# Moving the next tile's input transposes into the attention block, and a bf16 cast from VectorE to ScalarE, in a post-norm transformer layer on 8 cores

## The reference

```python
qkv = x @ W_qkv.T + b_qkv
q, k, v = jnp.split(qkv, 3, axis=-1)
q = q * HD ** (-0.5)
# q, k, v in blocks of 64 tokens, per head
attn = softmax(einsum('bhnld,bhnmd->bhnlm', qb, kb))
out = einsum('bhnlm,bhnmd->bhnld', attn, vb) @ W_out.T + b_out
x = layernorm(x + out)
h = silu(x @ wg.T) * (x @ wu.T)        # wg, wu = int32 / 127, hidden 3072
x = layernorm(x + h @ wd.T)
```

## Time and profile before

| | us |
|---|---|
| profiled execution | 2746.69 |
| its span, slowest core (core 0) | 2745.1 |
| median of the two timed runs | 2869.86 |
| the two timed runs | 2765.27 and 2974.46 |
| PE busy | 2001.0 (73% of the span) |
| DVE busy | 817.2 (30%) |
| ACT busy | 436.5 (16%) |

### The profile page before, as it was taken

How to read it: one execution, slowest core, us unless ns; L and a number is a source line. 1 busy time by engine, 2 the same in 40 slices (tenths; PEclk the granted TensorE clock), 3 DMA queues, 4 the chain that set the end, 5 groups by cost and what they waited for, 6 DMA issues and landing times.

```text
span 2745.1 us, 27109 instructions; the slowest of 8 cores (2723.5 to 2745.1 us)
## 1 busy us (share of the span) xinstructions
PE 2001.0 (73%) x10416; PEld 1001.5 (36%) x10560; DVE 817.2 (30%) x1314; ACT 436.5 (16%) x835; POOL 66.7 (2%) x111
## 2 busy tenths in 40 slices
PE   1666239657897669867797669876698678976795
PEld 1433114224443334324443335334443244433342
DVE  2444001153213341053312441143311532133411
ACT  0111101012211112021211112011211122111110
POOL 2000000100000000000000000000000000000000
PEclk9967569867898769966899679977799678987798
DMA  9999993810252004400153003410043102420033
GB/s 187 161 113 119 243 239 113 191 46 16 74 156 77 31 16 116 146 37 25 39 162 107 16 31 92 146 54 31 16 149 113 46 17 80 152 75 16 24 115 107
DMA packets 258829, 253.54 MB, mean 92 GB/s; under 512 B 88608, under 2 KB 221744, under 8 KB 258128
## 3 DMA queue, kind: packets, MB, share of 16 engines
q1 hardware_dynamic: 216576, 121.65, 17.1%
q0 software_dynamic: 19280, 86.11, 14.2%
q10 hardware_dynamic: 22848, 44.05, 4.8%
HBM read 216.13 MB, written 56.62 MB: 99 GB/s over the span
## 4 chain that ended last, share of the span: by engine, by line
PE 57%; DVE 13%; DMA 10%; SPq 9%; issue 5%; another core or an unknown queue 3%; ACT 2%; DVEq 0%; POOL 0%; ACTq 0%; POOLq 0%
PE ps L783 23%; PE ps L389 8%; SPq L289 7%; PE ps L838 7%; DMA wdb<-wdT_s 5%; PE ps L579 5%; PE ps L423 3%; PE ps L472 3%; PE ps L466 3%; DMA wdb<-wd_nat 2%; DVE x L861 1%; DVE stats L880 1%; SPq L263 1%; DVE stats L640 1%
## 5 line engine op out<-in xcount | busy, mean ns | idle before, releaser
L783 PE MATMUL ps<-x1T,wgu 128*128 128x512 bf16 x3008 | 664.4, 381 | 98.3 <-DMA wgu<-wuT_s 93.5
L783 PEld LDWEIGHTS ps<-x1T,wgu 128*128 128x128 bf16 x3072 | 301.4, 98 | 459.6 <-issue 102.1
L838 PE MATMUL ps<-wdb,hT 128*128 128x512 bf16 x1504 | 348.1, 385 | 62.3 <-DMA wdb<-wdT_s 34.0
L801 DVE TENSOR_TENSOR hT<-silu,ps 128x512 bf16<-128x512 bf16 x192 | 132.0, 687 | 753.7 <-PE ps L783 629.4
L389 PE MATMUL ps<-xT,RWqkv 128*128 128x256 bf16 x2048 | 266.0, 298 | 23.9 <-DVE xT L371 23.6
L838 PEld LDWEIGHTS ps<-wdb,hT 128*128 128x128 bf16 x1536 | 147.1, 99 | 263.2 <-issue 103.6
L389 PEld LDWEIGHTS ps<-xT,RWqkv 128*128 128x128 bf16 x2048 | 204.5, 106 | 85.1 <-issue 28.2
L423 PE MATMUL ps<-RWqkv,xT 128*128 128x512 bf16 x496 | 142.7, 435 | 87.6 <-DVE vtok L435 58.6
L579 PE MATMUL ps<-RWout,aoT 128*128 128x512 bf16 x480 | 166.0, 505 | 47.8 <-DVE aoT L567 25.0
L795 ACT ACTIVATE silu<-ps 128x512 bf16<-128x512 f32 x192 | 114.6, 597 | 520.1 <-PE ps L783 520.0
L397 ACT ACTIVATE qkT<-ps,bqkvT_s 128x256 bf16<-128x256 f32 x256 | 121.4, 474 | 454.7 <-PE ps L389 454.5
(11 more groups left out here) (71 smaller groups left out, 1067.8 us busy)
## 6 DMA issues: line engine op xcount, KB each, us to landing
wgu<-wgT_s SPq DMA_DIRECT2D x64, 768.0 KB, 4.9
wgu<-wuT_s SPq DMA_DIRECT2D x64, 768.0 KB, 7.0
wdb<-wdT_s ACTq DMA_DIRECT2D x84, 512.0 KB, 3.7
xf<-x POOLq DMA_DIRECT2D x16, 1024.0 KB, 5.2
y<-x POOLq DMA_DIRECT2D x16, 1024.0 KB, 5.8
x<-wqkv POOLq DMA_DIRECT2D x24, 512.0 KB, 9.1
wg_nat<-wg POOLq DMA_DIRECT2D x1, 6144.0 KB, 64.1
wu_nat<-wu POOLq DMA_DIRECT2D x1, 6144.0 KB, 120.9
```

Of the source, the lines that this page charges most:

```text
L783: P.do("tensor", lambda tn, wi=wi, k=k, mi_=mi_, boff=boff, pair=pair: tn.matmul(pair[:, wi * 512:(wi + 1) * 512], wgu[:, boff + wi * (KCH ...
L801: P.do("vector", lambda v, m=m, pair=pair: v.tensor_tensor(hT[:, m * 512:(m + 1) * 512], silu2[:, (m % 2) * 512:(m % 2 + 1) * 512], pair[: ...
L838: P.do("tensor", lambda tn, m=m, l=l, half=half, wslot=wslot, coff=coff: tn.matmul(psl[l][:, half * 512:(half + 1) * 512], hT[:, m * 512 + ...
```

## The change

`front_a` is cut in two. Its first part, now `front_x` (the cast of x, the transposes, the evacuations to `xT`), is emitted for tile t+1 inside `tile_front(t)`, between `attn_A(0, 1)` and `attn_T(0, 0)`. Its second part, `front_q` (q and k), stays where `front_a` was. For tile 0 both run ahead of the loop. The added argument `wait_scores` is a wait of TensorE on its own count, and by the rule above it emits nothing. The second edit moves the cast of the normalised x (L698 before) from VectorE to ScalarE, as an ACTIVATE with Copy, and the waits that go with it.

```diff
-            def front_a(t):
+            def front_x(t, wait_scores=0):
...
+                    if st == 0 and wait_scores:
+                        w.append(("pe", wait_scores))
...
+            def front_q(t):
                 for c in range(16):
...
                 attn_A(0, 0)
                 attn_A(0, 1)
+                if t + 1 < n_tiles:
+                    front_x(t + 1, wait_scores=mil["scores", t, 0, 1])
                 attn_T(0, 0)
...
-                    P.do("vector", lambda v, xsl=xsl, st=st: v.tensor_copy(
-                        out=aoT[:, st * 1024:(st + 1) * 1024], in_=xsl),
-                        inc="ve",
-                        waits=[("ve!", mil["norm1", t, st]), ("pe", mil["wout", t, 1]),
+                    P.do("scalar", lambda sC, xsl=xsl, st=st: sC.activation(
+                        out=aoT[:, st * 1024:(st + 1) * 1024], in_=xsl, func=AF.Copy),
+                        inc="sc",
+                        waits=[("ve", mil["norm1", t, st]), ("pe", mil["wout", t, 1]),
                                ("sb5", mil.get("dump_aoT", 0))])
-                    mil["x1b", t, st] = P.c["ve"]
+                    mil["x1b", t, st] = P.c["sc"]
...
-            front_a(0)
+            front_x(0)
+            front_q(0)
...
-                    front_a(2 * s + 1)
+                    front_q(2 * s + 1)
...
-                    front_a(2 * s + 2)
+                    front_q(2 * s + 2)
```

More of the change, by code:

```diff
@@ L624, in tile_front @@
                 if EARLY_A and t + 1 < n_tiles:
-                    front_a(t + 1)
+                    front_x(t + 1)
+                    front_q(t + 1)
                 if STAGE <= 7:
@@ L710, in tile_front @@
                             inc="pe" if c == KCH - 1 else None,
-                            waits=(w + [("ve", mil["x1b", t, st])]) if c == 0 else ())
+                            waits=(w + [("sc", mil["x1b", t, st])]) if c == 0 else ())
                     mil["x1t_mm", t, st] = P.c["pe"]
```

## The result

| | kernel before | changed kernel |
|---|---|---|
| profiled execution, us | 2746.69 | 2708.24 |
| its span, slowest core | 2745.1 (core 0) | 2706.7 (core 2) |
| median of all runs | 2758.82 (10 runs) | 2708.8 (11 runs) |
| ratio, with its 95% interval | 1 | 0.9843 (0.9822 to 0.9864) |
| DVE busy | 817.2 | 796.2 |

The change saves 1.6%, clear of the measurement's scatter and less than 2%. The forecast was 2712 us, a gain of 34.6 us. Some executions of either kernel run with a lower clock on one die and take some 8% longer (2974 before, 2931 after); the ratio leaves them out, and without that the median of the first two runs, 2869.86, cannot be understood.

The account below looks back on a forecast made before the run. TensorE's in-order list and its waits for VectorE were taken to bound the kernel. 13 tiles at 8.4 − 6.1 + 0.3 us plus 0.8 gave 34.6 us off 2746.7, so 2712 us, range 2685 to 2765.

Parts of the forecast that it names:

- The tail: From projection end to q/k: 8.4 us shorter per tile, about 7.6 from moving front_x and 0.8 from the cast's move.
- the cast's move: In the tail, casting the normalised x on ScalarE starts the first cast earlier, giving about 0.8 us a tile.
- The attention: Before the first attnT evacuation: VectorE's three inserted instructions and hops cost 6.1 us a tile, bounds 3.66 and 6.2.
- The lower bound of 3.66: In the attention: cost in us a tile of VectorE's three inserted instructions alone, with every hop hidden.
- The clock: TensorE's 1.2 GHz stretches in q/k and projections: 0.3 us a tile gained, bounds −1.25 and +1.8; projections keep their surroundings.
- The Trainium skill's advice: Slow matmul counts change from run to run, so do not fit them: clock term 0, forecast 2716 us.
- Tiles 0 and 1 don't count: What these tiles gain is lost in the first FFN's wait for its weights, so 13 tiles count in full.
- The sum: 13 x (8.4 − 6.1 + 0.3) + 0.8 = 34.6 us off the profiled 2746.7 us, so 2712 us.
- 1 (insertion eats the tail's gain): Insertion in the attention, through clock and hops, costs what the tail gives: 2725 to 2739 us; chance 0.15.
- 2 (projections slow to their end): TensorE stays at 1.2 GHz through both output projections, costing 4.0 us a tile: 2765 us; chance 0.05.
- 3, a table load: ScalarE's Copy cast needs table loads in the tail, 2 x 1.28 us a tile: 2746 us; chance 0.02.
- 4: Larger gain: attention hops hide behind VectorE (3.66, not 6.1) and the clock rises early: 2669 us; chance 0.10.

Follow-up runs that it names:

- e1: Kernel before with only the cast of the normalised x moved to ScalarE, front_a left whole: tail 19.00 us against 19.63, ratio 0.9947 to the kernel before.
- e2: Kernel before with only the input transposes moved, the cast staying on VectorE: tail 11.87 us, ratio 0.9865 to the kernel before.
- e3: Changed kernel with front_x's work done a second time in its old place in the tail: tile 94.96 us, median 2828.76 us.
- e4: Changed kernel with the cast of x put ahead of the first attn_A: v to attn_O 15.60 us, ratio 0.9693 to the kernel before.
- e5: e4 with the second half's input transposes sent to ps23 instead of ps01: v to attn_O 14.23 us, ratio 0.9699 to the kernel before.
- e8: Changed kernel run again unaltered, on the chip of e5 to e7: ratio 0.9858 to the kernel before, tile 86.78 us.
- e7: Changed kernel with front_x one step later, between attn_T(0, 1) and attn_O(0, 0): v to attn_O 19.52 us, ratio 0.9908 to the kernel before.
- e6: e5 with the next tile's q/k matmuls spread through the layer norm tail: tile 72.06 us, median 2534.62 us, ratio 0.9177 to the kernel before.

## Why the prediction was right, step by step

- *The tail, 8.4 us less.* Measured 8.40. Inside it the split was a little off: I gave the cast's move 0.8 and it is worth 0.63 (e1), and 7.6 to the transposes, which are worth 7.76 (e2). The ScalarE cast takes 1.048 us, as taken. But the pitch of the two groups of transposes is 1550.11 − 1547.51 = 2.60 and not 2.48, and the first group starts 0.1 us earlier and not 0.2: its cast begins 0.96 us after the normalisation does, where it was 1.45, and takes 0.36 us more. Together the two errors are 0.19 us. They are made up by a third: the row of q/k starts at 1550.91, 0.21 us before that of the transposes ends, and I had taken their end. That the tail came out at 8.4 all the same is luck. The 1.04 us worked out from the Trainium skill, "VectorE: DVE Perf Modes", an estimate, agrees with the row's 1.048. "ScalarE: Activation LUTs" of the Trainium skill names `relu`, `max`, `min`, `add` and `mul` as work for VectorE; one cast is indeed slower on ScalarE here (1.048 against 0.684), but that does not decide, since the first cast starts earlier by more than it loses and the second leaves the chain.
- *The attention, 6.1 us more.* Measured 6.06. That VectorE's list and the hops, and not PE's idle time, set this stretch is shown by e3 (the price alone, without the gain), e4 and e5 (each instruction or hop taken off VectorE's path gives its own length). The lower bound of 3.66 could be undercut: it counted the cast of x, 1.22 us, which e4 and e5 put where VectorE waited anyway, and e5 pays about 2.3 for the two evacuations that are left.
- *The clock, 0.3 us gained.* Measured 0.44 in the two projections and q/k together, and the windows show it piece by piece. In q/k the low stretch was 5.29 us; in the changed kernel the rows are

```profile
1522.08:1527.17 5.09, 5.09 (x12) 1.55 (x13) 2.60 (x9) 0.42 (x2) 0.00 (x0) 0.50 0.00 0
1534.01:1537.41 3.40, 3.40 (x8) 0.99 (x8) 0.00 (x0) 0.00 (x0) 0.00 (x0) 0.50 0.00 0
1550.91:1554.47 3.56, 3.56 (x19) 2.50 (x18) 1.23 (x1) 0.47 (x1) 0.00 (x0) 0.50 0.02 7
```

  for the first projection, the second and q/k. The granted clocks of all cores and tiles 2 to 14 give mean low stretches of 4.17, 3.49 and 4.86 us before and 4.93, 3.22 and 3.53 after. Half of each difference is +0.38, −0.13 and −0.67, against +0.35, −0.12 and −0.67 measured in these three stretches. So the clock explains these three stretches; the remaining 0.07 us of loss lies in the other rows of the table. My reason, that the projections keep their surroundings, was wrong for the first one, and 0.3 was a choice between the bounds and not a sum: that a loss of 0.35 and gains of 0.12 and 0.67 come out near it is in part luck. No run shows what sets the length of a low stretch.
- *The Trainium skill's advice* not to fit the number of slow matmuls ("TensorE: Matmul & The Clock Gate", Part 1) would have given 2716 and was not far off either. In the changed kernel the low stretch of q/k hardly varies: 3.53 us with a standard deviation of 0.14 over 104 passes (13 tiles, 8 cores), and 3.53 again in e8. Before, it scattered by 0.73, and there the advice fits better.
- *Tiles 0 and 1 don't count.* Right: the first FFN's wait grew by 3.7 us on the mean of the cores and its start did not move forward. VectorE's cast for tile 2 never waited for the load of x.
- *The sum.* 35.2 for 13 tiles against 33.8 forecast for them. The tail, the attention and the clock give 8.40 − 6.06 + 0.44 = 2.78 a tile, less the 0.07 above. The ratio of the forecast, (2746.7 − 34.6)/2746.7 = 0.987, lies 0.1% outside the interval of the first measurement and inside that of e8. What is left is within what the weight preparation and the FFN differ by between executions.
- *The rivals.* 1 (insertion eats the tail's gain) did not occur, since the first projection's low stretch grew by 0.76 us only and that of q/k shrank by 1.33. 2 (projections slow to their end) did not occur: the clock rose in both. It was priced too low: the core of the earlier trace rows has 17 of a projection's 18 matmul records, and the missing one is the first, so a half at 1.2 GHz is not 3.66 us but, on a core with all records, 1526.13 − 1522.08 = 4.05 in the changed kernel. With that the rival's time would be about 2773 and not 2765 (an estimate from these rows). 3, a table load, is excluded, since no load stands at the cast (L704: 32 casts, 1048 ns). 4 needed hidden hops; they are not hidden in this order, but e4 and e5 show that they can be.

## What to carry to other kernels

A wait of the busiest engine is a place for other work only if the engine it waits for has room too: here TensorE was idle in the attention, but VectorE was what it waited for, so the 7.6 us of moved work cost 6.1. Look first for independent work that is ready and needs only the waiting engine; the q/k matmuls were such work, ready that early only because `front_x` had been moved, and spread through the same tail they gave four times the change's gain in each tile (11.0 us against 2.7). When work is moved, ask in which list it stands ahead of whom, and who uses its PSUM buffer next (e7).

## What the runs showed of the hardware that was not expected

A gain in a stretch ahead of a restart of TensorE can come back in part as a longer stretch at 1.2 GHz. In e5 the attention is 1.37 us shorter than in e4, and the next projection 0.59 longer, because its low stretch grew from 4.18 to 5.37 us (means over tiles and cores). It can also go the other way: from the changed kernel to e4 that low stretch fell from 4.93 to 4.18. The clock at half speed costs half of such a stretch, and this was repeated in tile after tile. And the clock that the filled tail kept up did not last: in e6, on the slowest core, it is at 2.4 GHz from 1457.51 to 1488.23 and at 1.2 GHz from there to 1512.13, although PE's small matmuls for the scores stood back to back from 1485.48 to 1491.44. The projections' low stretches are 4.38 and 4.11 us there, no shorter than before.
